# Fetching the first half of a 128x512 operand in two transfers instead of one, at the very start of a graph-network kernel

## The reference

```python
x = _layernorm(x + _L0_gnn_ref(x, adj, W_self, W_neigh))  # x @ W_self + (adj @ x / rowsum(adj)) @ W_neigh
x = _layernorm(x + _L1_gnn_ref(x, adj, kernel, bias))     # relu(adj @ (x @ kernel) + bias)
x = _layernorm(x + _L2_gnn_ref(x, adj, W1, b1, W2, b2))   # relu(adj @ (.) @ W + b), twice
x = _layernorm(x + _L3_gnn_ref(x, adj, W, b))             # swish(adj @ (.) @ W + b), twice
```

## Time and profile before

| what | value |
| --- | --- |
| median of three runs | 1131.87 us |
| the profiled execution | 1131.75 us |
| its span | 1129.9 us |
| TensorE matmul busy | 1122.3 us (99%) |
| VectorE busy | 848.8 us (75%) |
| ScalarE busy | 620.5 us (55%) |
| read from HBM | 273.29 MB |

### The profile page before, as it was taken

How to read it: one execution, slowest core, us unless ns; L and a number is a source line. 1 busy time by engine, 2 the same in 40 slices (tenths; PEclk the granted TensorE clock), 3 DMA queues, 4 the chain that set the end, 5 groups by cost and what they waited for, 6 DMA issues and landing times.

```text
span 1129.9 us, 14459 instructions
## 1 busy us (share of the span) xinstructions
PE 1122.3 (99%) x5092; PEld 915.6 (81%) x5092; DVE 848.8 (75%) x1062; ACT 620.5 (55%) x866; POOL 55.3 (5%) x42
## 2 busy tenths in 40 slices
PE   9999999999999999999999999999999999999998
PEld 5567788888888888888888888888888888888886
DVE  6999999999898666775445497656587545677996
ACT  2365665666864444664444474444376545566884
POOL 0000000000021111000000010000000000000121
PEclk9999999999999999999999999999999999999999
DMA  9977776677967656596656588666668666787992
GB/s 365 377 283 246 259 239 219 214 228 226 310 242 275 191 187 223 200 354 194 215 186 199 181 296 288 199 215 200 215 221 320 204 207 187 256 329 278 331 333 90
DMA packets 82070, 276.34 MB, mean 245 GB/s; under 512 B 8784, under 2 KB 14416, under 8 KB 82000
## 3 DMA queue, kind: packets, MB, share of 16 engines
q1 hardware_dynamic: 75424, 270.57, 70.0%
q10 hardware_dynamic: 6576, 4.85, 1.5%
HBM read 273.29 MB, written 2.10 MB: 244 GB/s over the span
## 4 chain that ended last, share of the span: by engine, by line
PE 90%; DVE 5%; issue 2%; DMA 2%; ACT 0%; POOLq 0%; POOL 0%; DVEq 0%; ACTq 0%; SPq 0%
PE acc L521 28%; PE acc L522 28%; PE acc L526 28%; DVE deg_part L821 4%; PE acc L558 4%; DMA raw<-adj_tiles 2%; PE acc L509 1%; DVE adj_lo L961 1%; PE acc L536 1%; PE acc L544 0%; PE acc L611 0%; ACT adj_hi L796 0%; DVE deg_part L818 0%; DVE deg_sum L828 0%; POOLq L280 0%
## 5 line engine op out<-in xcount | busy, mean ns | idle before, releaser
L961 DVE TENSOR_TENSOR adj_lo<-raw,adj_hi 128x1024 fp32r<-128x1024 f32 x458 | 559.4, 1236 | 204.3 <-ACT adj_hi L796 188.8
L796 ACT CAST adj_hi<-raw 128x1024 fp32r<-128x1024 f32 x458 | 477.6, 1050 | 365.0 <-PE acc L526 341.4
L521 PE MATMUL acc<-adj_hi,op_hi 128*128 128x512 f32 x1422 | 560.2, 394 | 0.0
L522 PE MATMUL acc<-adj_hi,op_lo 128*128 128x512 f32 x1422 | 553.9, 390 | 0.0
L526 PE MATMUL acc<-adj_lo,op_hi 128*128 128x512 f32 x1422 | 438.3, 389 | 0.2
L526 PEld LDWEIGHTS acc<-adj_lo,op_hi 128*128 128x128 f32 x1422 | 266.8, 188 | 57.1 <-DVE adj_lo L961 1.1
L522 PEld LDWEIGHTS acc<-adj_hi,op_lo 128*128 128x128 f32 x1422 | 267.2, 188 | 54.3 <-issue 0.7
L521 PEld LDWEIGHTS acc<-adj_hi,op_hi 128*128 128x128 f32 x1422 | 267.2, 188 | 54.3 <-issue 0.7
L821 DVE TENSOR_TENSOR deg_part<-deg_part,raw 128x1024 f32<-128x1024 f32 x112 | 136.6, 1220 | 3.2 <-DMA raw<-adj_tiles 1.4
L985 POOL TENSOR_TENSOR rstd<-var_eps,minus_half 128x4 f32<-128x4 f32 x23 | 40.7, 1768 | 757.1 <-DVE var_eps L839 757.1
L652 ACT COPY t_agg<-acc 128x512 f32<-128x512 f32 x47 | 27.5, 585 | 64.3 <-PE acc L526 62.4
(11 more groups left out here) (85 smaller groups left out, 373.0 us busy)
## 6 DMA issues: line engine op xcount, KB each, us to landing
raw<-adj_tiles SPq DMA_DIRECT2D x511, 512.0 KB, 4.6
xt<-x_t ACTq DMA_DIRECT2D x8, 256.0 KB, 5.6
x_rows<-x_blocks SPq DMA_DIRECT2D x7, 256.0 KB, 9.5
out<-x_rows ACTq DMA_DIRECT2D x7, 256.0 KB, 5.6
raw<-adj_tiles SPq DMA_DIRECT2D x2, 256.0 KB, 3.8
x_rows<-x_blocks ACTq DMA_DIRECT2D x2, 128.0 KB, 4.0
out<-xt SPq DMA_DIRECT2D x2, 128.0 KB, 1.8
w<-W ACTq DMA_DIRECT2D x2, 64.0 KB, 3.9
```

Of the source, the lines that this page charges most:

```text
L521: nc.tensor.matmul(bank, op_block(op_hi, p, j), a_hi, start=first and b == 0, stop=False)
L522: nc.tensor.matmul(bank, op_block(op_lo, p, j), a_hi, start=False, stop=False)
L796: nc.scalar.copy(split_hi(s), raw[:, g % RAW, :]).then_inc(hi_ready, 1)
L961: nc.vector.tensor_tensor(split_lo(s), raw[:, g % RAW, :], split_hi(s).bitcast(fp32), ALU.subtract).then_inc(lo_ready, 1)
```

## The change

The first transfer of x (two blocks of 128 columns, 128 KB) becomes two transfers of one block each (64 KB). The second has a semaphore of its own, for which the second product of step 0 and ScalarE's cast wait. The remaining 128 KB stay one transfer and are now the third on ScalarE's queue.

```diff
         x_loaded = [sem(f"x_loaded{k}") for k in range(CHUNKS)]
+        x_second_loaded = sem("x_second_loaded")
         x_first_loaded = sem("x_first_loaded")
...
                 for b in range(BPT):
+                    if g == 0 and b == 1:
+                        pe.wait_ge(x_second_loaded, 16)
                     if g > 0:
                         pe.wait_ge(x_loaded[k], 16)
...
                 if k == STEPS[0][2]:
                     act.wait_ge(x_first_loaded, 16)
+                    act.wait_ge(x_second_loaded, 16)
                 act.wait_ge(x_loaded[k], 16)
...
             k = STEPS[0][2]
-            act.dma_start(cols(x_rows, k)[:, 0:2 * P], cols(x_blocks, k)[:, 0:2 * P]).then_inc(x_first_loaded, 16)
+            act.dma_start(cols(x_rows, k)[:, 0:P], cols(x_blocks, k)[:, 0:P]).then_inc(x_first_loaded, 16)
+            act.dma_start(cols(x_rows, k)[:, P:2 * P], cols(x_blocks, k)[:, P:2 * P]).then_inc(x_second_loaded, 16)
             act.dma_start(cols(x_rows, k)[:, 2 * P:CW], cols(x_blocks, k)[:, 2 * P:CW]).then_inc(x_loaded[k], 16)
```

## The result

The changed kernel takes 1133.25 us, the median of 21 executions, against 1131.83 us before (21 executions): 1.42 us more, a ratio of 1.0013 with a 95% interval of 1.0007 to 1.0019. Its executions scatter more as well: 1131.66 to 1136.30 us where those of before lie between 1131.48 and 1132.16. Two executions at a low mean granted clock, one of the 21 (1908.53 us at 0.556; the median of the other 20 is 1133.21) and one of the experiment with one transfer (1411.58 us at 0.753), are left out of the ratios and of all that follows.

The account below looks back on a forecast made before the run. TensorE bounds the kernel, transfers at most its beginning. Stream +0.06 us, with TensorE's +0.05 to +0.1 swallowed by the wait at 67.8, takes the profiled 1131.75 to 1131.81, or 1131.9 as median; range 1131.2 to 1132.8 us.

Parts of the forecast that it names:

- stream +0.06: Transfers behind x's first 128 KB: 288 packets instead of 144 make the stream 0.06 us later, the total's only net term.
- Part 1: Smaller first x transfer: the first product still starts when warm-up ends at 4.62; gain 0, at most 0.1 us.
- Part 2: Second x transfer and its new TensorE wait: lands at 5.1 to 5.4 us; cost 0, upper end 0.2 us.
- Part 3: Third x transfer, issued 0.45 us later, lands with tile 1 at 6.85 us (5.40 to 7.45); TensorE loses 0.05 to 0.1.
- What hides it: SP's queue, full beyond 15 us, and 1.3 us of VectorE idle time cover SP's refill and the degree sums being late.
- Part 4: Smaller packets for x's first 128 KB: the stream behind is 0.06 us later, bounds 0 and 0.1.
- Cover at 67.8: TensorE's wait for VectorE's degree sum at 67.8 us swallows its early 0.05 to 0.1 us, unless VectorE is late.
- Rival 2: VectorE's first degree sum and SP's refill: the third transfer's lateness is not hidden, 0.7 to 2.0 us; chance 0.07.
- Rival 3: TensorE before 5.4 us: a gap delays its clock's rise to 2.4 GHz, total 1134 to 1135 us; chance 0.02.
- My estimate from it, 1132.5: Start of the stream: by the skill page's 0.95 us per 64 KB, two small transfers add several tenths; total some 1132.5.
- my ring rows: Transfer queues' profile rows: 45 ns per 1 KB packet, 26 ns per 512 B packet, giving 0.06 us more stream.
- its rule that an engine drains a whole packet of one queue: DMA queues at the start: x would land ahead of SP's transfers, the third well before tile 1; under 0.1 us.

Follow-up runs that it names:

- one transfer: Against the kernel before, all 256 KB of x's first column in one transfer, for which first product and cast wait: 1131.70 us, ratio 1.0003.
- two pairs of traces: One trace each of the kernel before and the changed kernel, then both run again unedited: 1131.93 and 1133.29 us, ratios 1.0002 and 1.0011.
- Two transfers: Against the kernel before, x's first column in transfers of 64 then 192 KB, the second product waiting for the latter: 1132.57 us, ratio 1.0006.
- third on SP: Against the changed kernel, the 128 KB x transfer moved from ScalarE's queue to SP's, behind tile 0: 1132.69 us, ratio 1.0005 to the kernel before.
- 192 and 64: Against the kernel before, x's first column in transfers of 192 then 64 KB, waits unchanged; run twice: 1131.60 and 1131.81 us, both ratios 0.9997.
- waits joined: Against the changed kernel, the first product waits for both 64 KB transfers, the second product's own wait dropped: 1132.93 us, ratio 1.0005 to the kernel before.
- partitions run: Against the kernel before, x's first 128 KB cut by partitions into two 64 KB transfers, packets staying 1 KB: 1133.24 us, ratio 1.0015.
- filler: Against the changed kernel, eight more idle products of 128 columns between steps 0 and 1: 1132.97 us, ratio 1.0010 to the kernel before.

## Why the prediction was wrong

**The step that failed is the term "stream +0.06" of the sum, the lateness of tile 1 in parts 2 to 4.** I took its landing as fixed by bytes: what the early transfers save, the third brings, plus 0.06 us for more packets. Tile 1 came 1.2 and 1.9 us late in the two pairs of traces. My figure holds only while every DMA engine always has a packet to fetch, and in the changed kernel some had none.

Two things come together there. First, the transfers issued before tile 1 held 768 KB in the kernel before (256, 128, 256, 128) and 640 KB in the changed one; their last packet ended at 5.03 and at 4.33 us. Second, tile 1's packets came late to some engines. An estimate from the trace: an engine has eight packets of 4 KB of tile 1 to fetch, 0.16 us each, and eight of 1 KB of the third x transfer, 0.05 us each, and its signal came some 0.4 us behind its last packet. The two engines that signalled at 7.9 then began tile 1 near 5.8 us, over 4 us after its issue; in the trace of before all sixteen had begun it by about 5.0. So the two stood idle for some 1.4 us, half of it because their earlier work was shorter, half of it because the next packets came later than they had come before.

The bytes ahead alone do not give the loss. "Two transfers" and "third on SP" have the same 768 KB ahead of tile 1 as the kernel before, and have idle engines and a late tile 1; "192 and 64" and "one transfer" have 768 KB too and the time of before. By the table, a first x transfer of 64 KB goes with the loss, and a third transfer behind it seems to add to it (+0.8 with two, +1.4 to +1.5 with three).

The rows of before had a hint: TensorE's load at 6.76 and tile 1's landing at 6.65 stood 0.1 us apart, so that any lateness of tile 1 is TensorE's too. I had the pairs of landings, but never asked when a tile's packets start.

Point by point:

- *Part 1, the first product starts when the warm-up is through*: right, 4.62 again, though x's first block landed at 3.9. No gain from the earlier landing.
- *Part 2, the new wait costs nothing*: right; the block was there at 4.8, and without the wait the loss stays (waits joined).
- *Part 3, the third transfer lands with tile 1*: the pairing was right, 0.2 us behind it; the time was not, 8.1 instead of 6.85, beyond my upper bound of 7.45, as tile 1 itself moved; in the second trace it was 9.1. The degree sum came at 9.57, not 8.3, and SP's refill at 10.9, not 9.6.
- *What hides it*: SP's late refill was hidden, as tiles were in line. VectorE's idle time of 1.3 us was, as expected, partly used: 0.58 and 0.21 us of it were left before 17.49 and 18.93. But the tiles themselves were late, and no idle time of VectorE covers that.
- *Part 4, packets*: 0.06 us stays unmeasured; tile 1 at 8.4 in the partitions run shows that its lateness needs no 512-byte packets of x.
- *Cover at 67.8*: I counted on VectorE being on time. It was 1.14 us late there. What the early waits took back was 0.4 of 1.4 us in one trace and 1.8 of 3.85 us in the other.
- *Rival 2* had the size (0.7 to 2.0 us) with a chance of 0.07, and ended where the result did. Its condition came true as well, the third transfer landed behind 7.45 and the first degree sum was 2.7 us late; but that lateness did not bind, as VectorE still had 0.58 and 0.21 us of waiting for tiles left. What bound were TensorE's step 1 and the late tiles. *Rival 3*, the clock, is real, but behind the gap at 6.6 us and not ahead of 5.4; it shows in one of two traces of the changed kernel.
- *The Trainium skill*, page "DMA: Bandwidth & Descriptors", section Bandwidth: it says that transfers under 64 KB are ruled by their descriptors, and its 0.95 us for 64 KB is of a transfer issued from GpSimd. My estimate from it, 1132.5, pointed the right way, while my ring rows did not; but the reason was another. The runs show that it is not the smallness as such (192 and 64 has the same 64 KB and loses nothing) but when the small one comes.
- *The Trainium skill*, same page, the part on arbitration under Queues, rings and completion order: I drew too much from its rule that an engine drains a whole packet of one queue before it turns to another. SP's transfers of the start have eight packets to an engine as well as the x transfers, so the rule does not put x ahead of them. The runs do speak against it, in another way: x landed 0.2 us behind SP's transfer of the same moment whether an engine's eight packets of x were of 1 KB (before) or of 2 KB (one transfer), where eight take 0.67 us, so it does not look as if an engine fetched them in one go behind SP's.

**What is settled and what is not.** Shown: the changed kernel is slower, twice, and tile 1 comes late on some engines whenever x begins with a transfer of 64 KB, whether or not there is a new wait, a third transfer, another queue or a small packet; the order 192 and 64 restores the time. Seen in the one trace of a kernel each time, and not in its medians: the idle engines, their lateness to 30 us, the clock. Argued only: that tile 1's packets come late because something limits them where they are generated. Why some engines get theirs so late, why a first transfer of 64 KB brings it about, and why SP's issue took 1.56 us just then (1.34 in the second trace of the changed kernel, 1.23 with the waits joined) was not tried. Nor is the share of the clock in the median known: the filler's median is 0.3 to 0.4 us below that of the changed kernel, which 11 executions can't tell from nothing.

## What to carry to other kernels

When a stream starts, ask of each transfer not only when its bytes are through but when its first packets start on every engine; until then the transfers ahead must keep that engine busy. Cutting the first transfer smaller to start sooner can pay only if the consumer is not held by something else (here the warm-up), and in this kernel it left engines idle behind it. If a first column must be cut, put the large piece first. And look at the last of a landing's sixteen signals: one late engine holds a whole 512 KB tile.

## What the runs showed of the hardware

- A DMA engine that fell behind at the start stayed behind while its line was full: the tile whose eighth signal was on time at 26.9 us had its last one 1.55 us late, 20 us after the engines had stood idle. In the second pair of traces the tiles 2 to 15 were all 1.9 to 2.0 us late.
- From issue to landing, a 512 KB tile issued third on its queue took 5.0 to 5.4 us with full engines (four traces) and 6.2 to 7.3 us in six where the first x transfer had 64 KB.
- TensorE stood still for about 1.9 us after 7 us and then ran at 1.2 GHz from 9.7 to 13.0 us; after a gap of 1.57 us in the other trace it kept 2.4 GHz. The same kernel can go either way.
